# A fused attention and mixture-of-experts layer on one core: a new table of tasks per step, up products turned round, paired weighings, six probability buffers

## The reference

```python
q, k, v = x @ Wq, x @ Wk, x @ Wv          # 16 query heads, 4 key heads, two halves of 16 each
q1, q2, k1, k2 = rope(halves of q and k)
a1 = softmax(q1 @ k1.T / 4 + causal); a2 = softmax(q2 @ k2.T / 4 + causal)
out = (a1 - lam * a2) @ v
out = (out - mean) * rsqrt(var + EPS) * gn_w + gn_b     # var per head over the whole sequence
x = layernorm(x + 0.8 * out @ Wo)
e = argmax(x @ router.T); gate = sigmoid(max(x @ router.T))   # 8 experts, one per token
routed = silu_mul((x * gate) @ w_gate_up[e]) @ w_down[e]
shared = silu_mul(x @ shared_gate_up) @ shared_down
x = layernorm(x + routed + shared)
```

## Time and profile before

| | us |
|---|---|
| median of 3 runs | 854.79 |
| lowest and highest | 852.37 and 856.72 |
| profiled execution, its time | 854.18 |
| profiled execution, its span | 852.4 |

### The profile page before, as it was taken

How to read it: one execution, slowest core, us unless ns; L and a number is a source line. 1 busy time by engine, 2 the same in 40 slices (tenths; PEclk the granted TensorE clock), 3 DMA queues, 4 the chain that set the end, 5 groups by cost and what they waited for, 6 DMA issues and landing times.

```text
span 852.4 us, 10350 instructions
## 1 busy us (share of the span) xinstructions
PE 755.7 (89%) x3430; PEld 369.7 (43%) x3430; DVE 463.6 (54%) x1040; ACT 330.5 (39%) x607; POOL 305.2 (36%) x263
## 2 busy tenths in 40 slices
PE   7488899997699989977999899889999799999994
PEld 3243334333244433532444334434326555666662
DVE  2766986751667775416677655566425342333332
ACT  2414544434465433154554232554663002222220
POOL 3057511122982012029821130221240034666653
PEclk9778999999899999996899899999999999999998
DMA  3695085002038210020272100700067012221100
GB/s 128 149 335 149 5 197 88 28 2 38 0 70 178 41 55 3 22 42 1 63 161 41 55 4 2 210 2 1 2 207 293 25 44 63 60 60 62 46 22 1
DMA packets 51748, 62.95 MB, mean 74 GB/s; under 512 B 11303, under 2 KB 42797, under 8 KB 49840
## 3 DMA queue, kind: packets, MB, share of 16 engines
q1 hardware_dynamic: 42992, 49.29, 23.4%
q0 software_dynamic: 3824, 6.83, 2.7%
q10 hardware_dynamic: 4880, 6.16, 2.3%
HBM read 42.59 MB, written 22.41 MB: 76 GB/s over the span
## 4 chain that ended last, share of the span: by engine, by line
PE 71%; DVE 10%; POOL 6%; issue 4%; DMA 4%; ACT 2%; SPq 1%; POOLq 0%; DVEq 0%; ACTq 0%
PE pv_ps L964 15%; PE wide_ps L1042 9%; PE wide_ps L950 7%; PE s_ps L803 7%; PE wide_ps L791 5%; DVE mneg L1405 4%; PE wide_ps L934 4%; PE s_ps L835 3%; PE wide_ps L906 3%; PE s_ps L804 3%; PE pv_ps L1061 2%; PE misc L1061 2%; PE misc L881 2%; DMA k_parts<-w_exp 2%; PE wide_ps L939 2%
## 5 line engine op out<-in xcount | busy, mean ns | idle before, releaser
L1405 DVE TENSOR_REDUCE mneg<-s_ps 128x1 f32<-128x384 f32 (+3 forms) x352 | 216.7, 638 | 98.9 <-PE s_ps L804 94.9
L1178 ACT ACTIVATE w_exp<-wide_ps 128x512 f32<-128x512 f32 x320 | 180.0, 599 | 120.6 <-PE wide_ps L950 118.8
L964 PE MATMUL pv_ps<-w_exp,work 128*64 128x512 f32 x640 | 180.5, 644 | 10.0 <-POOL w_exp L1317 8.0
L1317 POOL TENSOR_SCALAR_AFFINE_SELECT w_exp<-w_exp 128x1024 f32<-128x1024 f32 x64 | 70.8, 1106 | 287.1 <-ACT w_exp L1178 287.1
L803 PE MATMUL s_ps<-w_exp 96*128 96x256 bf16 (+3 forms) x512 | 131.6, 316 | 20.7 <-DVE mneg L1405 13.2
L950 PE MATMUL wide_ps<-w_exp 98*128 98x512 bf16 x320 | 124.5, 398 | 13.2 <-ACT w_exp L1178 11.9
L950 PEld LDWEIGHTS wide_ps<-w_exp 98*128 98x128 bf16 x320 | 31.9, 103 | 155.5 <-ACT w_exp L1178 98.4
L804 PE MATMUL s_ps<-mask,identb 128*128 128x128 bf16 (+2 forms) x352 | 89.6, 254 | 0.0
L1042 PE MATMUL wide_ps<-w_exp,tables 128*128 x184 | 82.8, 592 | 0.0
L803 PEld LDWEIGHTS s_ps<-w_exp 96*128 96x128 bf16 x512 | 46.2, 101 | 70.9 <-DVE mneg L1405 43.0
L1196 ACT COPY work<-pv_ps 128x512 f32<-128x512 f32 x64 | 37.5, 585 | 58.1 <-PE pv_ps L964 57.2
(11 more groups left out here) (164 smaller groups left out, 982.5 us busy)
## 6 DMA issues: line engine op xcount, KB each, us to landing
w_exp<-q_parts SPq DMA_DIRECT2D x96, 128.0 KB, 5.0
w_exp<-w_up_in SPq DMA_DIRECT2D x8, 1024.0 KB, 8.9
slot_tokens<-x ACTq DMA_DIRECT2D x1, 4864.0 KB, 20.8
work<-x_in SPq DMA_DIRECT2D x8, 512.0 KB, 7.2
w_exp<-w_down_in SPq DMA_DIRECT2D x8, 512.0 KB, 9.6
q_parts<-w_exp SPq DMA_DIRECT2D x6, 512.0 KB, 6.0
w_exp<-k_parts SPq DMA_DIRECT2D x18, 128.0 KB, 3.7
gated_rows<-work SPq DMA_DIRECT2D x4, 512.0 KB
```

The costliest lines, as they stand in the source:

```text
L964: last = nc.tensor.matmul(pv_ps[s * 64:(s + 1) * 64, :], vo[:, kt, g, :], probs[:, n % NP, s, :], start=(kt == 0), stop=(kt == qt))
L1178: nc.scalar.activation(probs[:, n % NP, s], st_bank(v), ACT.Exp, scale=float(DH) ** -0.5).then_inc(st_done, 1)
L1317: nc.gpsimd.affine_select(out=e, in_=e, compare_op=ALU.is_ge, fill=0.0, base=0, pattern=[[0, 8], [1, P]], channel_multiplier=-1).then_inc( ...
L1405: nc.vector.tensor_reduce(out=mneg[:, qt, rows[0]:rows[-1] + 1], in_=s_ps[:, (v - 1) % 2, 0:len(rows) * w].rearrange("p (r k) -> p r k", r ...
```

## The change

It has five parts.

1. **Experts.** The up product is turned round: 128 columns of the expert's matrix are the weights, and the 128 tokens move, so the hidden layer comes out with its features on partitions. The four transposes and ScalarE's copy go. The down weights alone stay in w_exp from before; the up weights (1 MB) are loaded per tile, by the owner that SP reads, into a ring of four.
2. **Weighings.** In query tiles 1 and 3 the weighings of an even and of the following odd key tile are done one right after the other.
3. **Six probability buffers** instead of four.
4. **Boundary.** The eight preps, the mean, the squares and their sums stand interleaved in BOUNDARY; after the last boundary there are no preps.
5. **Table.** Tasks may stand in the middle of a step, ahead of the weighing, or at its end; nearly all have new steps. PREP_LATER starts one step later and ends at step 14 instead of 11. The first bank of the next sequence moves from step 19 to 20.

x2 becomes a ring of two sequences to make room.

```diff
-NP = 4
+NP = 6
+RINGUP = 4
+WEIGHED = [[m for m in (n - 2, n - 1) if m >= 0 and m + (2 if STEPS[m][0] % 2 and STEPS[m][2] % 2 == 0 else 1) == n] for n in range(NSTEP + 1)]
-    here = [(2, 0, 8), (3, 8, 19)] if first else [(3, 3, 19)]
-    for back, rows in ((0, here), (-1, [(0, 19, 22), (1, 22, 28), (2, 28, 40)])):
+    here = [(2, 0, 9), (3, 9, 18)] if first else [(3, 2, 20)]
+    for back, rows in ((0, here), (-1, [(0, 20, 22), (1, 22, 28), (2, 28, 39)])):
...
-TASKS[0].append(("mean", 0, 1))
-TASKS[1].append(("square", 0, 1))
-TASKS[2].extend([("sum_squares", 0, 1), ("sum_squares", 1, 1)])
-TASKS[3].extend([("sum_squares", 2, 1), ("sum_squares", 3, 1)])
-TASKS[4].append(("var", 0, 1))
-for _qt in range(QT):
-    for _i, _name in enumerate(PER_TILE):
-        TASKS[6 + 5 * _qt + _i].append((_name, _qt, 1))
+put(1, END, ("var", 0, 1))
+put(2, END, ("norm", 0, 0))
+put(3, END, ("norm", 1, 0), ("scale", 0, 1), ("scale", 1, 1), ("turn", 0, 1))
+put(4, END, ("norm", 2, 0), ("project", 0, 1))
+put(5, END, ("norm", 3, 0), ("x2", 0, 1))
...
+put(9, MID, ("turn", 1, 1))
+put(9, END, ("project", 1, 1))
...
+put(13, END, ("norm", 7, 0), ("turn", 2, 1))
+put(14, END, ("project", 2, 1))
...
-BOUNDARY = [("v", 0, 0), ("norm", NUNIT - 1, 1), ("sum", QT - 1, 1)]
+BOUNDARY = [("v", 0, 0), ("prep", 0, 0), ("prep", 1, 0), ("norm", 15, 1), ("prep", 2, 0), ("prep", 3, 0), ("sum", 3, 1), ("mean", 0, 1),
+            ("prep", 4, 0), ("square", 0, 1), ("sum_squares", 0, 1), ("sum_squares", 1, 1), ("prep", 5, 0), ("square", 1, 1), ("prep", 6, 0), ("prep", 7, 0), ("sum_squares", 2, 1), ("sum_squares", 3, 1)]
...
-PREP_LATER = [0, 0, 1, 1, 2, 3, 3, 4, 4, 5, 6, 6, 7, 8, 8, 9, 10, 11]
+PREP_LATER = [1, 3, 3, 3, 4, 5, 5, 6, 6, 7, 7, 7, 9, 10, 10, 11, 13, 14]
...
+            def load_upper(i):
+                if i >= RINGUP:
+                    sp.wait_ge(up_full, 2 * (i - RINGUP + 1))
+                e = sp.value_load(owner[0:1, i:i + 1], min_val=0, max_val=E - 1)
+                sp.dma_start(w_upper[:, i % RINGUP], w_up.rearrange("e k n -> (e k) n")[bass.ds(e * D, D)].rearrange("(c p) n -> p c n", p=P)
+                             ).then_inc(upper_loaded[i % RINGUP], 16)
...
+                        if part == 1:
+                            for name, arg, back in tasks_at(n, MID, prep_next, post):
+                                task(name, arg, b - back)
+                        if part == 1:
+                            for m in WEIGHED[n]:
+                                weigh(b, m)
...
                 for half in range(2):
-                    for ch in range(DC):
-                        w = w_exp[:, bass.ds(e * WEXP + ch * 2 * F + half * F, F)]
-                        last = nc.tensor.matmul(up_ps[:, r, half, :], xeT[:, r, ch, :], w, start=(ch == 0), stop=(ch == DC - 1))
+                    for fc in range(F // P):
+                        for ch in range(DC):
+                            w = w_upper[:, i % RINGUP, ch, half * F + fc * P:half * F + (fc + 1) * P]
+                            last = nc.tensor.matmul(up_ps[:, r, half, fc * P:(fc + 1) * P], w, xeT[:, r, ch, :], start=(ch == 0), stop=(ch == DC - 1))
                     last.then_inc(up_full, 1)
...
             for i in range(NROUTE):
-                following = owner_of(i + 1) if i + 1 < NROUTE else None
-                turn_hidden(i)
+                held = owner_of(i)
                 if i + 2 < NROUTE:
                     turn_tile(i + 2)
-                if following is not None:
-                    up(i + 1, following)
+                if i + 1 < NROUTE:
+                    up(i + 1)
                 down(i, held)
```

More of the change, by code:

```diff
@@ L117, in banks_at @@
     return [x for x in (BANKS_LATER if b else BANKS_FIRST).get(n, []) if x[2] == 0 or b < B - 1]
[L120 to L129, removed]
+MID, END = 0, 1
+TASKS = {(n, half): [] for n in range(NSTEP) for half in (MID, END)}
@@ L133, with put @@
+def put(n, half, *tasks):
+    TASKS[n, half].extend(tasks)
 PER_TILE = ("turn", "project", "x2", "retake", "logits")
 SHARED = [(name, fc) for fc in range(F // P) for name in ("shared_gate", "shared_up")] + [("shared_down", t) for t in range(QT)]
-for _qt in range(QT - 1):
-    TASKS[FIRST_ST[_qt + 1] + 2].append(("sum", _qt, 0))
-TASKS[0].append(("mean", 0, 1))
-TASKS[1].append(("square", 0, 1))
-TASKS[2].extend([("sum_squares", 0, 1), ("sum_squares", 1, 1)])
-TASKS[3].extend([("sum_squares", 2, 1), ("sum_squares", 3, 1)])
@@ new lines @@
+put(12, END, ("logits", 1, 1))
+put(13, END, ("norm", 7, 0), ("turn", 2, 1))
+put(14, END, ("project", 2, 1))
+put(15, END, ("sum", 1, 0))
+put(16, MID, ("x2", 2, 1))
+put(16, END, ("norm", 8, 0), ("retake", 2, 1))
+put(17, END, ("logits", 2, 1))
+put(18, MID, ("turn", 3, 1))
+put(19, MID, ("project", 3, 1))
+put(19, END, ("mt", 3, 0), ("x2", 3, 1))
+put(20, MID, ("norm", 9, 0))
+put(20, END, ("retake", 3, 1), ("bias", 0, 0))
+put(21, END, ("logits", 3, 1))
+put(22, MID, ("top", 0, 1))
+put(22, END, ("norm", 10, 0))
@@ L174, with tasks_at @@
 ONCE = (("bias", 0), ("mt", 2))
-def tasks_at(n, ahead, post):
-    return [t for t in TASKS[n] if (t[2] == 0 and not (t[:2] in ONCE and post)) or (t[2] < 0 and ahead)
+def tasks_at(n, half, ahead, post):
+    return [t for t in TASKS[n, half] if (t[2] == 0 and not (t[:2] in ONCE and post)) or (t[2] < 0 and ahead)
             or (t[2] > 0 and post and (ahead or t[:2] not in SHARED))]
 def body_tasks(ahead, post):
-    return [t for n in range(NSTEP) for t in tasks_at(n, ahead, post)]
+    return [t for n in range(NSTEP) for half in (MID, END) for t in tasks_at(n, half, ahead, post)]
 NEAR_TASKS = ("v", "mt", "norm")
@@ L757, in _ @@
             sp.wait_ge(owners_done, 1)
+            load_upper(0)
             sp.wait_ge(tokens_scattered, NTOK * 16)
-            for i in range(ID_GROUPS[2][1]):
+            for i in range(2):
+                load_ids(i)
+            load_upper(1)
+            load_upper(2)
+            for i in range(2, ID_GROUPS[2][1]):
                 load_ids(i)
@@ L762, in _ @@
             store_x2s(B - 1)
-            for i in range(ID_GROUPS[2][1], NROUTE):
-                load_ids(i)
+            load_upper(3)
+            later = list(range(ID_GROUPS[2][1], NROUTE))
+            for i in range(RINGUP, NROUTE):
+                for _ in range(5):
+                    if later:
+                        load_ids(later.pop(0))
+                load_upper(i)
             for r in range(2):
@@ L910, in task @@
                     for ch in range(DC):
-                        last = nc.tensor.transpose(here[:, ch * P:(ch + 1) * P], x2[:, b * QT + arg, ch * P:(ch + 1) * P], ident[:])
+                        last = nc.tensor.transpose(here[:, ch * P:(ch + 1) * P], x2[:, b % 2 * QT + arg, ch * P:(ch + 1) * P], ident[:])
                 elif name == "logits":
@@ L968, in body @@
             def body(b, prep_next, post):
-                if prep_next and b > 0:
-                    for k in range(ST_PREP):
-                        prep(b, k)
                 for s in range(2):
@@ L1151, in task @@
                 if name == "shared_gate":
-                    if arg == 0:
-                        act.wait_ge(gated_done, b + 1)
                     act.wait_ge(far_full, v)
@@ L1166, in body @@
             def body(b, prep, post):
-                if prep and b > 0:
-                    for k in range(ST_PREP):
-                        evacuate(b, k)
                 for n in range(NSTEP):
@@ L1184, in body @@
                         cast(b + 1, part, pair)
-                for name, arg, back in tasks_at(NSTEP - 1, prep, post):
+                for name, arg, back in tasks_at(NSTEP - 1, END, prep, post):
                     task(name, arg, b - back)
@@ L1222, in boundary @@
             def boundary(b):
-                for name, arg, back in BOUNDARY:
+                for name, arg, back in boundary_tasks(b < B - 1):
                     task(name, arg, b - back)
```

179 lines of the change are left out of this document (97 added, 82 removed).

## The result

The changed kernel takes 828.54 us (median of 4 runs, 824.92 to 831.14) where the kernel before, run beside it, takes 853.58 (4 runs, 851.92 to 856.72): a ratio of 0.9712, 95% interval 0.9666 to 0.9757. The forecast was 821 with a range of 805 to 841, so it is 7.5 us too optimistic and inside the range. The profiled execution of the changed kernel took 831.14 us, its span is 829.4 against 852.4.

What follows compares the result with a forecast made beforehand. TensorE was taken to bound the kernel (89% busy), with GpSimd pacing the first twelve steps of sequences 1 and 2. From 854.2 us: experts -9, sequence 1 -8.5, sequence 2 -10.5, sequence 0 -3, sequence 3 -2 give 821, range 805 to 841.

Steps and rivals of the forecast that it cites:

- Experts, forecast 9: Experts: turned up products shorten first up product to last down product by 9.5 us, less 0.5 charged for token lists.
- The step of the tile: Experts: a tile takes 5.50 us instead of 5.82, its up product being 32 records of 0.111 us.
- rival D: Experts: weight loads don't hide behind matmuls, a tile takes 8.9 us, 902 us in all; chance 0.02.
- rival C: Experts: up weights come late, at 160 GB/s a tile takes 9.0 us, 903 us in all; chance 0.05.
- 0.5 us for the token lists: Start of experts: token lists land up to 3 us later behind the first up load; shared products hide most.
- Pairs, forecast 8 gained: Query tiles 1 and 3: each pair of weighings saves 0.25 us where TensorE sets the pace.
- The marginal price: Weighings: the second of two adjacent ones adds 0.86 us, where a lone one costs 1.10.
- The wait that I named: Tile 3 of sequence 3: TensorE waits some 0.2 us after a pair, so 1 us gained there instead of 3.
- Sequences 1 and 2, forecast 19: Boundary, buffers and table: better GpSimd order, pairs and task places gain 8.5 us in sequence 1, 10.5 in sequence 2.
- The bank's wait of 1 us: Step 20 of sequence 1: TensorE arrives at about 271.8, the last split's data at 272.7, so it waits a microsecond.
- Sequence 3, forecast 2 gained: Statistics come first, fourth weighing 2.2 us later at 1.86 us a unit; won back later, with pairs -2, bounds +3 and -5.
- rival A: Sequences 1 and 2: GpSimd and the DMAs keep the turn, 3 us gained in each, 834 us; chance 0.18.

Runs made afterwards that it cites:

- e7: Changed kernel with single weighings, the fourth up load issued behind four more token lists, and the last product added before the next-to-last tile is normalized: 822.28 us.
- e9: Changed kernel with the old steps of the preparation (PREP_LATER) put back, nothing else undone: 843.60 us, ratio 0.9898.
- e11: Kernel before the change with the new PREP_LATER alone: 858.36 us, ratio 1.0069.
- e10: Changed kernel with mean, squares and sums back in steps 0 to 3 and the variance in step 4, for all sequences after the first: 834.14 us.
- e3: Changed kernel with mean, squares and their sums back in steps 0 to 3 of the last sequence alone: 827.92 us, ratio 0.9715.
- e2: Changed kernel with four probability buffers instead of six: 826.48 us, ratio 0.9704.
- e8: e7 with the statistics of the last sequence placed as in e3: 818.58 us, ratio 0.9598.
- e6: Changed kernel with paired weighings in query tile 1 alone, tile 3 weighing singly: 826.67 us, ratio 0.9703.
- e1: Changed kernel with every weighing alone, one step after its own, no pairs: 822.99 us, ratio 0.9655.

## Why the prediction was right, and where it was off

*Experts, forecast 9, measured 5.5.* The step of the tile was right: 5.50 forecast, 5.52 on average over the middle tiles, with 32 records in 3.58 us (732.42 to 736.00). The up product ran at one record per 0.112 us with a weight load each, PEld busy for 103 of 108 us beside PE for 108. So the loads overlapped throughout, and rival D is refuted in the kernel itself. What the Trainium skill says in TensorE: Matmul & The Clock Gate, Part 3, that loads overlap only across different row groups, doesn't agree with this. The same part of that page also names the background weight buffer as a target for which a load is pulled ahead, which the prediction passed over; no run here shows which buffer these loads go to. The up loads landed 5.1 us after issue (median) and no up product waited for one; rival C is refuted, with 224 GB/s over the stretch at a DMA share of 0.65. The mis-sized terms are at the ends. From the first up to the last down product I had 124.4 us. It was 127.3 (125.7 to 127.9 in the profiles without e7's edit), and 124.8 with the load of the fourth ring slot issued later (e7). I had charged 0.5 us for the token lists that come behind the loads and looked at the first tile alone. It was the third tile's tokens that came late and held up the second up product, for 2.26 us. Another 1.1 us is lost at the very end (14.6 us for 13.5), for which I had no term. VectorE finishes the tile before the last before it adds the last one; the other order gives back 0.6 of it (e7), the rest is open.

*Pairs, forecast 8 gained (3 in sequence 0, 2 each in 1 and 2, 1 in 3), measured 5 lost.* This step failed. The marginal price was right (0.86 us for the second one). The wait that I named was another, for exponentials, only in sequence 3 and at 0.2 us. The runs showed in its place waits for VectorE, up to 1.46 us long: for the maxima, and for the shared products' factors. With the pairs out, sequence 0 gains 1.4 us over before, near the low end of my 0 to 5.

*Sequences 1 and 2, forecast 19, measured 20.3.* The total is right, but in part by luck. The reason given holds up to step 20: 5.6 us were forecast there in each, 4.1 and 6.6 were measured, and undoing GpSimd's order alone takes 13.3 us away (e9). With the old order step 20 comes 86.6 and 86.7 us after the value product, later than in the kernel before, so the other edits cost a little there. The mask of step 11 ended at 247.6 (forecast: near 247). From step 20 on I had 3 us each, 2 of them for pairs. Measured were 4.2 and 5.4, although the pairs cost 2.5 there: the new places of the tasks must have given 6.7 and 7.9 us where I had put 1. This error and that of the pairs cancelled. Which of the moved tasks gives it was not tried; the table and rows under the result show where it lies.
Two things more were off and cancelled. The last split ended at 261.0 instead of 254.5, since GpSimd waited 3.43 us for an exponential and 2.52 for a cast meanwhile. The way from there to the bank was 13.7 us, not 18.2. The bank's wait of 1 us that I forecast didn't come. That the later splits are dangerous e11 bears out: there they made the kernel before slower. Hiding the statistics under the preps is worth 2.7 and 3.5 us (e10), for which I had said 4 to 5 of steps.
Some numbers of the working are not what the rows give, without effect on the forecast: 278.66 less 272.7 is 6.0 and not 5.6, the DMA share beside 130 GB/s is 0.95 and not 0.97, and for the 13 us that TensorE alone could gain no row is given.

*Sequence 3, forecast 2 gained, measured 2.7 lost.* The exponentials started 11.6 us after the first value product, not 3.6: 8 us later, where I forecast 7. The step that failed is the one behind it, that the weighings catch up at 1.86 us a unit and the fourth comes only 2.2 us later than before. It came 9.3 us later, 26.3 us after the first value product (512.90) instead of 17.1, at 4.9, 4.4 and 3.0 us a unit:

```profile
526.87 1.98 PE L1022 MATMUL pv_ps<-w_exp,work 128*64 128x512 f32 x4 [0.16 <-POOL w_exp L1355]
531.79 1.98 PE L1022 MATMUL pv_ps<-w_exp,work 128*64 128x512 f32 x4
536.23 1.08 PE L1022 MATMUL pv_ps<-w_exp,work 128*64 128x512 f32 x4
539.22 1.08 PE L1022 MATMUL pv_ps<-w_exp,work 128*64 128x512 f32 x4
```

The first two ran at half clock (1.98 us for 1.08). I hadn't priced the clock, which was 0.74 in the first 12 us, where TensorE was busy for 5.32, and 0.66 in the next 16. Of the 9.3 us, 6.6 were won back later. With the statistics in the steps the sequence takes 103.2 us, 3.2 under before (e3), and 104.0 in e10. That is more than the 2 I forecast for the whole.

*Six buffers*, for which I had no term of their own but let the exponentials run ahead: nothing (e2).

The measured 828.54 lies between the forecast and rival A (834), but not for A's reasons: its two sequences came as forecast. The profiled execution is 10 us above the forecast, and these lie in sequences 0 and 3 and in the experts.

## What to carry to other kernels

Work that is ready but not urgent is what an engine fills its waits with. Batching it saves its switching cost and takes the filler away; before batching, look at the stretch for waits of the engine itself, not only at its busy share.
A helper engine's order matters most where it paces. Changing it moves the last piece too, so the consumer of the last piece has to move with it: the same order gained 13 us over two sequences in one table and lost 4 in the other.
A stretch that costs little because something else covers it (the statistics under the preps) must be looked at separately in the iteration where the cover is missing.

## What I had not expected of the hardware

The granted clock goes with differences of the size studied here. Four executions of the changed kernel took 824.92 and 826.54 us at a mean granted clock of 0.963 and 0.961, and 830.54 and 831.14 at 0.955. The tail took 65.2 to 68.9 us by the number of stretches at 1.2 GHz in it. Which edit brings such a stretch stays open: e3 and e10 had two in the tail, e8 with the same edit one, e6 without it two. Below some 3 us a stage of a single profile says nothing unless its clock is read beside it, while stages that stay at 2.4 GHz repeat closely (steps 26 to 39 of sequence 1 take 46.28, 46.29, 46.30 and 46.29 us in e1, e6, e7 and e8).
